# Planned attention and FP4 feed-forward block on one core: shifted due times, a split planned in four jobs, value eviction moved to ScalarE, paired mask matmuls

## The chip, the core and the metric

The kernel runs on one core of a Trainium2 chip. The metric is the device time of one execution in microseconds (us), as a median over runs. Engines: PE is TensorE's matmul, PEld its weight load, DVE is VectorE, ACT is ScalarE, POOL is GpSimd, SP is SyncE (here the only issuer of DMAs, each engine working through its own list in order).

## What is computed

One transformer block with adaptive layer norm, for x of 16 batches x 1024 tokens x 256 features in float32. Cut to what matters:

```
sa, ca, ga, sb, cb, gb = split(silu(c) @ wmod)          # per batch, |ga|,|gb| >= 0.25
h = layernorm(x) * (1 + ca) + sa
Q, K, V = h @ q_w.T + q_b, h @ k_w.T + k_b, h @ v_w.T + v_b   # 16 heads of 16
p = softmax(Q K / 4 + slope_h * (k - q), causal)
x = x + ga * ((p @ V) @ o_w.T + o_b)
h = layernorm(x) * (1 + cb) + sb
g = silu(fp4(h) @ fp4(w_gate).T) * (fp4(h) @ fp4(w_up).T)     # 704 wide
x = x + gb * (fp4(g) @ fp4(w_down).T)                         # fp4: blocks of 16, quantised and back
```

Since the rows of a softmax sum to 1, a constant added to V comes out of the attention unchanged.

## The kernel before

**One list per engine, written by a planner.** `plan()` names every job of all 16 batches: its engine, a cost, a due time, what it comes after, and a lag until others see it. `settle()` places them one by one: of all jobs that are ready it takes the one with the smallest pair (start, due), where the start is the later of the engine's free time and the job's own, but at least the free time plus 0.05, so that jobs that can start within 0.05 us are ranked by due time. The result, `PLAN.order`, is what each engine's `run()` walks through, in order, with semaphore waits. Nothing is decided on the chip. Batches overlap: in the stretch in which batch b is in attention, the projections of b+1 and the feed-forward of b-1 run as well. The length of a batch in due times is L = 240.

**Rings.** TensorE's results go through rings to the engine that evicts them: ring A to ACT (up to 4 jobs ahead), ring D to DVE (3 ahead), and Q passes quantised tiles from DVE to POOL (2 ahead). The evictor takes them in the order in which TensorE filled them. `RINGS`, `APART`, `BANKS` and `AHEAD` stand at the head of class Plan. `APART` names the DVE jobs that the planner does not start while a POOL job is under way, and the other way round (`memory` in `settle()`).

**The jobs of one batch.** TR and U (L730, L738) transpose the normed x and project it to q and k in four units u; ACT evicts a U into xa (L888). POOL splits each unit into three bf16 parts (`split`, L970 to L976: high part, rest, middle part, last part, four instructions of 128x1024 that wait for one another) as one job SPL of cost 6.5. SP moves the parts into the rows of qa and ka (MOVE, L561). V (L769) projects the values in two halves of 128x1024; **DVE** evicts each by four 128x256 additions of `bv_row` into `va` (L1161), and `va_ready` tells TensorE. S (L713) computes scores with queries on the partitions, 22 jobs for each of four groups g of four heads, and DVE takes the row maxima (L1101 for several heads at once, L1103 for one). SM, MT and TOP turn the maxima into three more rows of qa. T (L673) computes the scores again, transposed, ACT takes their exponential into one of three slots of `arena` (L874), and PV (L690) multiplies them with va. A T or S job whose block holds the diagonal adds the causal mask by a matmul of the identity with a mask of 128 columns: L676 behind each head of a T job, L718 behind each head of an S job. T jobs hold one, two or four heads (at 512 or 384, 256 and 128 columns); with four, one 512-column mask goes first (L669). S jobs of the second query tile (qt = 1) hold four heads of 256 columns, side by side, each with a mask of its own; those of qt = 2 and 3 two heads, in a bank each. CO (L853) evicts the sums; DEN, NUM, RDW and RBC are DMAs, RD (L1127) DVE's reciprocal of the sums, MUL (L1018) POOL's normalising. O (L781) is the output projection with weights scaled by ga (WG, L993); OB (L989) scales the bias `bo_row` by ga, and FOLD adds it to x. In the feed-forward, per pair of tiles r: LN, XR, XQ on DVE (L1186 to L1077), XQ on POOL (L1008, L1011), XT; per tile t: GA with silu on ACT (L800, L912), UP (L807, L1213), HR and HQ on DVE (L1066 to L1077), HQ on POOL, HT, DN (L823, L1219), RES. SP waits for MT before it issues TOP (L565).

Of the kernel before, what the change touches and what calls it, by code (L numbers as in the profile page):

```python
# [19 lines left out]
G = 4  # L20
# [60 lines left out]
class Plan:  # L81
# [6 lines left out]
    APART = ("LN", "XR", "XQ", "HR", "HQ", "N3", "SM", "WQ", "QROW")  # L88
# [6 lines left out]
    def add(self, engine, event, cost, due, *after, lag=0.06, ring=None, takes=None, lock=None, banks=0, holder=None):  # L95

        self.jobs[engine, event] = (cost, due, [a for a in after if a], lag, ring, takes, lock, banks)
        if banks:  # L100
            self.holder[event] = holder or (self.RINGS[ring][1], event)

    def settle(self):
# [30 lines left out]
        while ready:  # L134
            best = None
            places = {n: place(n) for n in (1, 2)}
            for key in ready:
# [22 lines left out]
                rank = (max(t, start + 0.05), due)  # L160
# [36 lines left out]
def plan():  # L197
# [9 lines left out]
    def projections(b, at):  # L207
# [13 lines left out]
        for u in range(4):  # L221
            for hf in range(2):
# [6 lines left out]
            p.add("POOL", ("SPL", b, u), 6.5, due, ("ACT", ("U", b, u, 0)), ("ACT", ("U", b, u, 1)),  # L229
                  ("POOL", ("SPL", b, u - 1)) if u else ("POOL", ("SPL", b - 1, 3)), *free)  # L230
        for u, g in ((0, 0), (1, 0), (0, 1), (1, 1), (2, 2), (3, 2), (2, 3), (3, 3)):
            p.add("SP", ("MOVE", b, u, g), 3.9, at + (g + 1) * L / NG, ("POOL", ("SPL", b, u)),
                  ("PE", ("T", b - 1, g, NS - 1, jobs_of(NS - 1) - 1)), ("SP", ("TOP", b - 1, g + 1)) if g + 1 < NG else None, lag=6.0)
        for v in range(2):
            pe(("V", b, v), 3.5, at + L, ("ACT", ("TR", b, 0, 1)), ("ACT", ("TR", b, 1, 1)),
               ("ACT", ("T", b - 1, NG - 1, NS - 1, jobs_of(NS - 1) - 1)), ("PE", ("V", b, 0)) if v else None, ring="D", on="DVE",
               takes_cost=1.75, banks=2, then=(("PE", ("PV", b - 1, NG - 1, NS - 1)),))

    def maxima(b, at):
        n, last = 0, ("PE", ("S", b - 1, NG - 1, NT - 1))  # L240
        for g in range(NG):
            for j, (qt, _, heads) in enumerate(TILES):
                w = (qt + 1) * P
                due = at + L * n / (NG * sum(h * (q + 1) * P for q, _, h in TILES)) - 30.0
                pe(("S", b, g, j), 0.65 if qt == 0 else heads * (cols(w) + 0.11) if w <= BANK else cols(BANK) + cols(w - BANK), due, last,
# [12 lines left out]
    def attention(b, at):  # L258
        n, last = 0, ("PE", ("T", b - 1, NG - 1, NS - 1, jobs_of(NS - 1) - 1))
        for g in range(NG):  # L260
            for s in range(NS):
                w = span(s)[1]
                heads = together(s)
                for i in range(jobs_of(s)):
                    due = at + L * n / (NG * NS * G)
                    old = b * NG * NS + n // G - P_SLOTS
                    pe(("T", b, g, s, i), 0.63 if heads == G else heads * (cols(w) + (0.1 if s in DIAGONAL else 0.0)) + 0.01, due, last,
# [7 lines left out]
                      ("PE", ("PV", b, g, s - 1)) if s else None, ("DVE", ("V", b, 1)) if (g, s) == (0, 0) else None, lag=0.22,  # L275
# [18 lines left out]
    def weights():  # L294
# [15 lines left out]
    def residual(b, at):  # L310

        p.add("SP", ("GROW", b), 0.7, at, ("POOL", ("WG", b - 1)), lag=3.0)
        p.add("POOL", ("OB", b), 0.75, at + 10.0, ("SP", ("GROW", b)), ("POOL", ("FOLD", b - 1, NPAIR - 1)))
# [63 lines left out]
def adaln_block(nc, x, wq, bq, wk, bk, wv, bv, wo, bo, w_gu, w_down, cond, w_mod, out):  # L377
# [5 lines left out]
    with ExitStack() as ctx:  # L383
# [40 lines left out]
        bv_row, bo_row = sb("bv_row", [P, D]), sb("bo_row", [P, D])  # L424
# [36 lines left out]
        va_ready = sem("va_ready")  # L461
# [3 lines left out]
        xn_ready = sem("xn_ready")  # L465
# [31 lines left out]
        def _(sp):  # L497
# [14 lines left out]
            for dst, src in ((bv_row, bv), (bo_row, bo)):  # L512
                sp.dma_start(dst[:, :], src.broadcast_to((P, D))).then_inc(w_in[4], 16)
# [98 lines left out]
        def _(pe):  # L612
# [44 lines left out]
            def run():  # L657
                for e in PLAN.order["PE"]:
                    kind, b = e[0], e[1]
                    if kind == "T":  # L660
# [10 lines left out]
                        for m in range(heads):  # L671
                            h = j * heads + m
                            mm = pe.matmul(ps[:, m * w:(m + 1) * w], ka[g][0:KT, h, kt * P:(kt + 1) * P], qa[g][0:KT, h, q0:q0 + w],  # L673
                                           start=heads < G, stop=heads == G or s not in DIAGONAL, skip_group_check=True)
                            if s in DIAGONAL and heads < G:
                                mm = pe.matmul(ps[:, m * w:m * w + P], identb[:, :], maskT[:, :], start=False, stop=True,  # L676
                                               skip_group_check=True)
                        mm.then_inc(a_full, 1)
                    elif kind == "PV":
# [6 lines left out]
                        if g == 0 and s == 0:  # L686
                            pe.wait_ge(va_ready, b + 1)
# [6 lines left out]
                    elif kind == "S":  # L694
# [11 lines left out]
                        if qt == 0:  # L706
                            pe.matmul(ps[:, :], identb[:, :], triangle.unsqueeze(1).broadcast_to((P, G, P)),
                                      start=True, stop=False, skip_group_check=True)
                        for m in range(heads):
                            for a in range(0, w, BANK):  # L710
# [3 lines left out]
                                               ka[g][0:KS, h0 + m, a:z], start=qt > 0, stop=qt == 0 or heads == 1,  # L714
# [47 lines left out]
                    elif kind == "V":  # L762
# [4 lines left out]
                        for t in range(4):  # L767
                            for c in range(C):
                                mm = pe.matmul(ps[:, t * D:(t + 1) * D], featT[:, c, (4 * half + t) * P:(4 * half + t + 1) * P],  # L769
                                               wvT[:, c, :], start=(c == 0), stop=(c == C - 1))  # L770
                        mm.then_inc(d_full, 1)
# [60 lines left out]
        def _(act):  # L832
# [10 lines left out]
            def run():  # L843
                for e in PLAN.order["ACT"]:
# [19 lines left out]
                    if kind == "T":  # L864
# [62 lines left out]
        def _(pool):  # L927
# [31 lines left out]
            def split(b, u):  # L959
                dst = parts[PART_SLOT[u]]  # L960
                if u == 3:
                    for g in (0, 1):
                        pool.wait_ge(part_in[0, g], b * 96 + 96)
                elif b:
                    old = (3, 1, 2)[u]
                    for g in (2 * (old // 2), 2 * (old // 2) + 1):
                        pool.wait_ge(part_in[old, g], b * 96)
                pool.wait_ge(a_free, max(in_a["U", b, u, hf] for hf in range(2)))
                done = b * 4 + u + 1
                nc.gpsimd.tensor_scalar(dst[:, 0, :], qk[u % 2], 1.0, 1.0, ALU.mult, ALU.mult).then_inc(high_done, 1)  # L970
                pool.wait_ge(high_done, done)
                nc.gpsimd.tensor_tensor(qk[u % 2], qk[u % 2], dst[:, 0, :], ALU.subtract).then_inc(rest_done, 1)
                pool.wait_ge(rest_done, done)
# [347 lines left out]
```

## Time and profile before

| | us |
|---|---|
| median of 3 runs (3885.79 to 3888.7) | 3885.8 |
| the profiled execution, its own time | 3883.8 |
| its span, first to last instruction | 3881.4 |
| PE busy | 3570.4 (92%) |
| DVE busy | 3109.8 (80%) |
| ACT busy | 1902.2 (49%) |
| POOL busy | 1285.0 (33%) |

A matmul's busy time runs to the modelled end of its result, and matmuls overlap, so start-to-start times say more of TensorE's pace than durations. "Idle before" is what ended an engine's idle time just before a group. The mean granted TensorE clock was 0.98 of full speed.

### The profile page before, as it was taken

Reading aid. Unit: us, or ns where it says so; the run is one execution under the profiler, and the core shown is the slowest. Engines: PE = TensorE matmul, PEld = TensorE weight load, DVE = VectorE, ACT = ScalarE, POOL = GpSimd, SP = SyncE. Lnnn points to the kernel's source line nnn. Section 1 sums busy time; section 2 is a strip of 40 time slices with the busy share of each in tenths; the row PEclk is TensorE's granted clock in tenths of the full one; section 3 lists DMA queues with packets and bytes.
Section 4 is the critical chain, followed back from the end, with each engine's and each line's share of the span. In section 5 each row is a group of like instructions: output and inputs, shape, how many; then the busy total and the mean of one; then the engine's idle time right before and its main releaser. Section 6 shows DMA issues by size and latency. Waiting matters only on the chain.

```text
span 3881.4 us, 57828 instructions
## 1 busy us (share of the span) xinstructions
PE 3570.4 (92%) x21300; PEld 1882.3 (48%) x21300; DVE 3109.8 (80%) x6061; ACT 1902.2 (49%) x3471; POOL 1285.0 (33%) x918
## 2 busy tenths in 40 slices
PE   5999999999999999999999999999999999999967
PEld 2334454544555554455544555455455545444435
DVE  9888779788887878879787887878878787877745
ACT  2455545455554545545445444554545454554521
POOL 5214234142332414324242332514334242332223
PEclk7899999999999999999999999999999999999988
DMA  7251323332342331333332242332333233232000
GB/s 125 35 95 34 67 48 53 61 48 49 55 66 49 59 57 35 65 55 52 57 55 48 49 70 48 56 60 38 60 56 58 49 61 52 39 61 39 20 25 11
DMA packets 158188, 205.51 MB, mean 53 GB/s; under 512 B 44036, under 2 KB 98004, under 8 KB 157908
## 3 DMA queue, kind: packets, MB, share of 16 engines
q1 hardware_dynamic: 157908, 201.82, 30.7%
q8 instruction: 170, 2.79, 0.3%
q14 instruction: 110, 0.90, 0.1%
HBM read 63.78 MB, written 17.89 MB: 21 GB/s over the span
## 4 chain that ended last, share of the span: by engine, by line
PE 68%; DVE 15%; ACT 9%; issue 3%; DMA 3%; SPq 3%; POOL 0%; POOLq 0%; ACTq 0%; DVEq 0%
PE banks L690 12%; PE banks L713 10%; PE banks L673 10%; PE banks L800 7%; PE banks L823 7%; PE banks L807 7%; ACT arena L874 6%; DVE banks L1103 3%; PE banks L738 3%; PE banks L781 3%; PE banks L769 3%; SPq L561 2%; DMA sums<-oT 2%; PE banks L816 2%; PE banks L676 2%
## 5 line engine op out<-in xcount | busy, mean ns | idle before, releaser
L874 ACT ACTIVATE arena<-banks 128x512 f32<-128x512 f32 (+1 forms) x2432 | 1274.4, 582 | 1008.1 <-PE banks L676 597.0
L1103 DVE CUSTOM_DVE_ANT_0 banks<-banks,mask 128x640 f32<-128x640 f32 (+3 forms) x1024 | 1033.3, 1043 | 123.7 <-PE banks L713 115.1
L673 PE MATMUL banks<-qa,ka 105*128 105x512 bf16 (+3 forms) x3072 | 817.0, 329 | 119.9 <-ACT arena L874 100.2
L713 PE MATMUL banks<-ka,qa 102*128 102x512 bf16 (+3 forms) x3072 | 753.0, 331 | 38.6 <-DVE top L1103 18.6
L690 PE MATMUL banks<-arena,va 128*17 128x512 f32 (+3 forms) x6144 | 643.7, 493 | 18.8 <-ACT arena L874 15.2
L673 PEld LDWEIGHTS banks<-qa,ka 105*128 105x128 bf16 x3072 | 279.7, 97 | 684.4 <-ACT arena L874 436.0
L1008 POOL TENSOR_TENSOR hid<-hid,tm 128x704 f32<-128x704 f32 x128 | 214.6, 1677 | 727.5 <-DVE hid L1077 727.5
L1101 DVE TENSOR_REDUCE top<-banks 128x2 f32<-128x768 f32 (+3 forms) x384 | 387.6, 1040 | 79.8 <-PE banks L718 75.8
L713 PEld LDWEIGHTS banks<-ka,qa 102*128 102x128 bf16 x3072 | 260.0, 99 | 379.0 <-DVE top L1103 106.6
L823 PE MATMUL banks<-wdT,hqT 128*128 128x256 f32 x1536 | 368.4, 391 | 2.8 <-ACT hqT L917 2.8
L1022 POOL TENSOR_TENSOR xr<-xr,delta 128x256 f32<-128x256 f32 x128 | 103.7, 810 | 675.7 <-DVE delta L1219 675.7
L800 PE MATMUL banks<-wguT,xqT 128*128 128x352 f32 x1024 | 326.7, 463 | 0.7 <-ACT xqT L908 0.7
L807 PE MATMUL banks<-wguT,xqT 128*128 128x352 f32 x1024 | 326.3, 464 | 0.0
L823 PEld LDWEIGHTS banks<-wdT,hqT 128*128 128x128 f32 x1536 | 292.5, 194 | 66.8 <-ACT hqT L917 9.7
L676 PE MATMUL banks<-maskT,identb 128*128 128x128 bf16 x1536 | 320.1, 220 | 0.0
L807 PEld LDWEIGHTS banks<-wguT,xqT 128*128 128x128 f32 x1024 | 191.4, 191 | 107.9 <-issue 5.4
L1213 DVE TENSOR_TENSOR hid<-hid,banks 128x704 f32<-128x704 f32 x128 | 112.8, 886 | 158.0 <-PE banks L807 157.3
L800 PEld LDWEIGHTS banks<-wguT,xqT 128*128 128x128 f32 x1024 | 189.7, 191 | 94.7 <-ACT arena L874 2.6
L912 ACT ACTIVATE hid<-banks 128x352 f32<-128x352 f32 x256 | 117.2, 463 | 237.6 <-PE banks L800 236.9
L690 PEld LDWEIGHTS banks<-arena,va 128*17 128x17 f32 x6144 | 104.2, 95 | 237.7 <-ACT arena L874 127.3
L1008 POOL TENSOR_TENSOR xb<-xb,tm 128x512 f32<-128x512 f32 x64 | 81.5, 1273 | 353.2 <-DVE xb L1077 353.2
L917 ACT COPY hqT<-banks 128x512 f32<-128x512 f32 (+1 forms) x256 | 110.9, 489 | 161.8 <-PE banks L816 161.8
(146 smaller groups left out, 4703.8 us busy)
## 6 DMA issues: line engine op xcount, KB each, us to landing
qa<-parts SPq DMA_DIRECT2D x384, 128.0 KB, 4.5
ka<-parts SPq DMA_DIRECT2D x384, 128.0 KB, 5.2
xa<-in_x SPq DMA_DIRECT2D x16, 1024.0 KB, 9.9
rsumT<-rsum_dram SPq DMA_DIRECT2D x64, 256.0 KB
onT<-oT SPq DMA_DIRECT2D x256, 64.0 KB, 4.3
xr<-in_x SPq DMA_DIRECT2D x64, 256.0 KB, 2.7
out_x<-xr SPq DMA_DIRECT2D x64, 256.0 KB, 2.2
ffn_rows<-rows_dram SPq DMA_DIRECT2D x16, 384.0 KB, 7.3
```

The source lines that it names most:

```text
L673: mm = pe.matmul(ps[:, m * w:(m + 1) * w], ka[g][0:KT, h, kt * P:(kt + 1) * P], qa[g][0:KT, h, q0:q0 + w], start=heads < G, stop=heads == ...
L676: mm = pe.matmul(ps[:, m * w:m * w + P], identb[:, :], maskT[:, :], start=False, stop=True, skip_group_check=True)
L690: mm = pe.matmul(out[32 * h:32 * h + VW, :], va[:, kt, g * G + h, :], probs[:, s % P_SLOTS, h, 0:w], start=s in FIRST, stop=s in LAST, ski ...
L713: mm = pe.matmul(ps[:, at:at + z - a], qa[g][0:KS, h0 + m, qt * P:(qt + 1) * P], ka[g][0:KS, h0 + m, a:z], start=qt > 0, stop=qt == 0 or h ...
L800: mm = pe.matmul(ps[:, 0:FH], src[:, c, :], wguT[:, c, e[3] * FH:(e[3] + 1) * FH], start=(c == 0), stop=(c == C - 1))
L807: mm = pe.matmul(ps[:, k * BANK:k * BANK + FH], src[:, c, :], wguT[:, c, FF + k * FH:FF + (k + 1) * FH], start=(c == 0), stop=(c == C - 1))
L823: mm = pe.matmul(ps[:, 0:D], hqT[t % 2][:, c, :], wdT[:, c, :], start=(c == 0), stop=(c == FC - 1))
L874: nc.scalar.activation(probs[:, s % P_SLOTS, j * heads:(j + 1) * heads, 0:w], ps[:, 0:heads * w].rearrange("p (h q) -> p h q", h=heads), A ...
L912: nc.scalar.activation(hid[t % 2][:, k * FH:(k + 1) * FH], ps[:, 0:FH], ACT.Silu).then_inc(a_free, 1)
L1008: nc.gpsimd.tensor_tensor(u, u, m, ALU.subtract).then_inc(gridded, 1)
L1101: nc.vector.tensor_reduce(tops, ps, AX.X, ALU.max).then_inc(d_free, 1)
L1103: nc.vector.tensor_tensor_reduce(out=ps, in0=ps, in1=mask[:, S - w:S], scale=1.0, scalar=MASKED, op0=ALU.add, op1=ALU.max, accum_out=tops) ...
```

## The change

It has five parts. (1) A table `SHIFT` adds a constant to the due time of each kind of job on each engine, and `PATIENCE` replaces the 0.05 in the rank: 0 on PE and DVE, 0.8 on ACT, 0.05 on POOL, 0.3 on SP. (2) N2 and LR (the two reciprocal-root chains) join `APART`. (3) POOL's split is planned as four jobs of one instruction each, so that others may stand between them. (4) V goes through ring A: ACT evicts each half by one 128x1024 copy, without the bias; the bias goes once, at the start, through the output projection (BB copies the bias column into `delta[0]`, BO multiplies it with o_w, DVE adds the result to `bo_row`), and OB of batch 0 waits for that. PV waits for ACT's copy itself; `va_ready` is gone. (5) The masks of two heads that lie side by side in a bank are one 256-column matmul: in T jobs of two heads, and for heads in pairs in S jobs of qt = 1. Only the first matmul of such a pair or job starts a new accumulation.

```
-    APART = ("LN", "XR", "XQ", "HR", "HQ", "N3", "SM", "WQ", "QROW")
+    APART = ("LN", "XR", "XQ", "HR", "HQ", "N2", "N3", "LR", "SM", "WQ", "QROW")
+    SHIFT = {"ACT CO": 12.0, "ACT GA": -20.0, "ACT HT": -16.0, "ACT T": -12.0, "ACT TR": 22.0, "ACT U": 11.0,
+             "ACT XT": 16.0, "DVE DN": 1.0, "DVE HQ": -14.0, "DVE LN": 12.0, "DVE LR": -24.0, "DVE N1": 1.0, "DVE N2": -1.0,
+             "DVE N3": 8.0, "DVE O": -3.0, "DVE RD": 17.0, "DVE S": -20.0, "DVE SM": -21.0, "DVE XQ": 11.0, "DVE XR": -22.0,
+             "PE DN": 10.0, "PE GA": 32.0, "PE HT": -7.0, "PE TR": 21.0, "PE U": 4.0, "PE UP": -7.0, "PE V": 1.0,
+             "PE XT": 9.0, "POOL FOLD": -2.0, "POOL HIGH": 13.0, "POOL HQ": 4.0, "POOL MID": -26.0, "POOL MUL": -6.0,
+             "POOL RES": 8.0, "POOL REST": -6.0, "POOL SPL": -2.0, "POOL WG": 8.0, "POOL XQ": 1.0, "SP MOVE": 10.0,
+             "SP NUM": -1.0, "SP OUT": -4.0, "SP RDW": 25.0, "SP XIN": 14.0}
+    PATIENCE = {"ACT": 0.8, "POOL": 0.05, "SP": 0.3}
...
+        due += self.SHIFT.get(engine + " " + event[0], 0.0)
...
-                rank = (max(t, start + 0.05), due)
+                rank = (max(t, start + self.PATIENCE.get(key[0], 0.0)), due)
...
-            p.add("POOL", ("SPL", b, u), 6.5, due, ("ACT", ("U", b, u, 0)), ("ACT", ("U", b, u, 1)),
+            p.add("POOL", ("HIGH", b, u), 1.1, due, ("ACT", ("U", b, u, 0)), ("ACT", ("U", b, u, 1)),
                   ("POOL", ("SPL", b, u - 1)) if u else ("POOL", ("SPL", b - 1, 3)), *free)
+            p.add("POOL", ("REST", b, u), 2.2, due, ("POOL", ("HIGH", b, u)))
+            p.add("POOL", ("MID", b, u), 1.1, due, ("POOL", ("REST", b, u)))
+            p.add("POOL", ("SPL", b, u), 2.2, due, ("POOL", ("MID", b, u)))
...
-               ("ACT", ("T", b - 1, NG - 1, NS - 1, jobs_of(NS - 1) - 1)), ("PE", ("V", b, 0)) if v else None, ring="D", on="DVE",
-               takes_cost=1.75, banks=2, then=(("PE", ("PV", b - 1, NG - 1, NS - 1)),))
+               ("ACT", ("T", b - 1, NG - 1, NS - 1, jobs_of(NS - 1) - 1)), ("PE", ("V", b, 0)) if v else None, ring="A", on="ACT",
+               takes_cost=1.15, banks=2, then=(("PE", ("PV", b - 1, NG - 1, NS - 1)),))
...
+        p.add("DVE", ("BB", 0), 0.4, 30.0)
+        pe(("BO", 0), 0.95, 40.0, ("DVE", ("BB", 0)), ring="D", on="DVE", takes_cost=0.45)
...
# TensorE, a T job
-                                           start=heads < G, stop=heads == G or s not in DIAGONAL, skip_group_check=True)
-                            if s in DIAGONAL and heads < G:
-                                mm = pe.matmul(ps[:, m * w:m * w + P], identb[:, :], maskT[:, :], start=False, stop=True,
-                                               skip_group_check=True)
+                                           start=heads < G and m == 0, stop=heads == G or s not in DIAGONAL, skip_group_check=True)
+                        if s in DIAGONAL and heads < G:
+                            mm = pe.matmul(ps[:, 0:heads * w].rearrange("p (h q) -> p h q", h=heads)[:, :, 0:P], identb[:, :],
+                                           maskT[:, :].unsqueeze(1).broadcast_to((P, heads, P)), start=False, stop=True,
+                                           skip_group_check=True)
...
# TensorE, an S job
+                        paired = 2 if qt == 1 else 1
...
+                            if heads > 1 and qt > 0 and m % paired == paired - 1:
+                                at = (m + 1 - paired) * tile_pitch(heads, w)
+                                mm = pe.matmul(ps[:, at:at + paired * w].rearrange("p (h k) -> p h k", h=paired)[:, :, w - P:w], identb[:, :],
+                                               triangle.unsqueeze(1).broadcast_to((P, paired, P)), start=False, stop=True,
                                                skip_group_check=True)
-                            if heads > 1 and qt > 0:
-                                at = m * tile_pitch(heads, w) + w - P
-                                mm = pe.matmul(ps[:, at:at + P], identb[:, :], triangle, start=False, stop=True, skip_group_check=True)
...
# ScalarE
+                    if kind == "V":
+                        t = 4 * e[2]
+                        if b:
+                            act.wait_ge(pv_done, b * NG * NS)
+                        act.wait_ge(a_full, full)
+                        nc.scalar.copy(va[:, t:t + 4, :, 0:HD], ps.rearrange("p (t h w) -> p t h w", t=4, h=H)).then_inc(a_free, 1)
...
# VectorE
-                        for j in range(4):
-                            ins = nc.vector.tensor_tensor(va[:, t + j, :, 0:HD], ps[:, j, :, :],
-                                                          bv_row[:, :].rearrange("p (h w) -> p h w", h=H), ALU.add)
...
+                        nc.vector.tensor_tensor(bo_row[:, :], bo_row[:, :], bank(e)[:, 0:D], ALU.add).then_inc(d_free, 1)
```

## Rows read from the trace of the kernel before

**Rows 1.** The page: busy time, share of the span and instructions of each engine

```profile
PE 3570.4 (92%) x21300; PEld 1882.3 (48%) x21300; DVE 3109.8 (80%) x6061; ACT 1902.2 (49%) x3471; POOL 1285.0 (33%) x918
```

**Rows 2.** Windows; columns: stretch, length, busy of PE, PEld, DVE, ACT, POOL, PEclk, DMA share, GB/s

```profile
0.00:484.00 484.00, 410.14 (x2360) 188.93 (x2360) 404.31 (x879) 228.17 (x398) 154.13 (x110) 0.92 0.40 71
484.00:3388.00 2904.00, 2749.50 (x16665) 1457.85 (x16666) 2381.33 (x4585) 1478.96 (x2708) 992.58 (x703) 1.00 0.32 54
3388.00:3881.40 493.40, 410.72 (x2277) 235.53 (x2276) 324.18 (x599) 195.11 (x367) 138.30 (x105) 0.93 0.16 31
```

**Rows 3.** Windows of 50 us, the two of the first 1000 us that are compared

```profile
250.00:300.00 50.00, 49.52 (x364) 23.95 (x361) 38.48 (x76) 30.66 (x61) 5.73 (x5) 1.00 0.60 99
...
950.00:1000.00 50.00, 49.16 (x330) 29.40 (x329) 36.23 (x71) 23.65 (x44) 9.43 (x8) 1.00 0.38 63
```

**Rows 4.** The chain that ended last, shares of the span by engine

```profile
PE 68%; DVE 15%; ACT 9%; issue 3%; DMA 3%; SPq 3%; POOL 0%; POOLq 0%; ACTq 0%; DVEq 0%
```

**Rows 5.** Waits: engine, line, waited for: us in total, times, longest us

```profile
PEld banks L673 <- ACT arena L874: 436.0, 684, 2.1
...
PEld banks L690 <- ACT arena L874: 127.3, 342, 1.1
...
PEld banks L713 <- DVE top L1103: 106.6, 147, 3.1
...
DVE rsums L1127 <- DMA sums<-oT: 66.5, 38, 3.7
...
DVE va L1161 <- PE banks L769: 57.0, 30, 3.3
```

**Rows 6.** Groups of PE matmuls by form (busy, mean ns | idle before)

```profile
L823 PE MATMUL banks<-wdT,hqT 128*128 128x256 f32 x1536 | 368.4, 391 | 2.8 <-ACT hqT L917 2.8
...
L676 PE MATMUL banks<-maskT,identb 128*128 128x128 bf16 x1536 | 320.1, 220 | 0.0
L718 PE MATMUL banks<-mask,identb 128*128 128x128 bf16 x768 | 161.6, 222 | 0.0
```

**Rows 7.** Timeline of PE: start us, us, what, count

```profile
1116.14 2.75 PE L823 MATMUL banks<-wdT,hqT 128*128 128x256 f32 x12
1118.73 2.53 PE L800 MATMUL banks<-wguT,xqT 128*128 128x352 f32 x8
...
1128.04 0.27 PE L713 MATMUL banks<-ka,qa 102*128 102x256 bf16 x1
1128.15 0.22 PE L718 MATMUL banks<-mask,identb 128*128 128x128 bf16 x1
1128.21 0.27 PE L713 MATMUL banks<-ka,qa 102*128 102x256 bf16 x1
```

**Rows 8.** Groups: DVE's value eviction, and ACT's copies in two sizes

```profile
L1161 DVE TENSOR_TENSOR va<-banks,bv_row 128x256 f32<-128x256 f32 x128 | 45.3, 417 | 57.0 <-PE banks L769 57.0
...
L917 ACT COPY hqT<-banks 128x512 f32<-128x512 f32 x128 | 75.7, 591 | 161.8 <-PE banks L816 161.8
...
L917 ACT COPY hqT<-banks 128x256 f32<-128x256 f32 x128 | 49.6, 388 | 0.1
```

**Rows 9.** Two DVE lines: group (mean ns), then duration ns min/median/max of the same

```profile
L1073 DVE SCALAR_TENSOR_TENSOR hid<-hid,invH 128x704 f32<-128x704 f32 x128 | 143.6, 1122 | 1.9
...
L1108 DVE SCALAR_TENSOR_TENSOR top_rest<-top,top_parts 128x32 f32<-128x32 f32 x64 | 38.5, 602 | 2.2
...
L1073 DVE SCALAR_TENSOR_TENSOR hid<-hid,invH x128: 883/891/2737, 344.0 to 3864.3; 128x704 f32<-128x704 f32 x128
...
L1108 DVE SCALAR_TENSOR_TENSOR top_rest<-top,top_parts x64: 191/193/2304, 104.3 to 3670.0; 128x32 f32<-128x32 f32 x64
```

**Rows 10.** Timeline of POOL and of DVE at one place

```profile
1098.07 2.27 POOL L972 TENSOR_TENSOR xa<-xa,parts 128x1024 f32<-128x1024 f32 x1
1098.40 2.69 DVE L1077 TENSOR_TENSOR hid<-hid,tm 128x704 f32<-128x704 f32 x1
```

**Rows 11.** Waits of SP's queue: waited for, us in total, times, longest us

```profile
SPq L565 <- DVE topT L1120: 957.5, 64, 39.0
```

More of the change, by code:

```diff
@@ L266, in attention @@
                     old = b * NG * NS + n // G - P_SLOTS
-                    pe(("T", b, g, s, i), 0.63 if heads == G else heads * (cols(w) + (0.1 if s in DIAGONAL else 0.0)) + 0.01, due, last,
+                    pe(("T", b, g, s, i), 0.63 if heads == G else heads * cols(w) + (0.11 if s in DIAGONAL else 0.01), due, last,
                        ("SP", ("TOP", b, g)) if (s, i) == (0, 0) else None, ring="A", on="ACT",
@@ L770, in run @@
                                                wvT[:, c, :], start=(c == 0), stop=(c == C - 1))
+                        mm.then_inc(a_full, 1)
+                    elif kind == "BO":
+                        ps = open_banks(e)
+                        pe.wait_ge(bv_ready, 1)
+                        for c in range(C):
+                            mm = pe.matmul(ps[:, 0:D], delta[0][:, c * P:(c + 1) * P], woT[:, c, :], start=(c == 0), stop=(c == C - 1))
                         mm.then_inc(d_full, 1)
@@ L957, in _ @@
             nc.gpsimd.memset(wdT[:, FC - 1, :], 0.0).then_inc(pad_clear, 1)
[L959 to L973, printed above, removed]
-                nc.gpsimd.tensor_scalar(dst[:, 1, :], qk[u % 2], 1.0, 1.0, ALU.mult, ALU.mult).then_inc(mid_done, 1)
-                pool.wait_ge(mid_done, done)
-                nc.gpsimd.tensor_tensor(dst[:, 2, :], qk[u % 2], dst[:, 1, :], ALU.subtract).then_inc(split_done, 1)
             def run():
@@ L980, in run @@
                     kind, b = e[0], e[1]
-                    if kind == "SPL":
-                        split(b, e[2])
+                    if kind in ("HIGH", "REST", "MID", "SPL"):
+                        u = e[2]
+                        dst, src, done = parts[PART_SLOT[u]], qk[u % 2], b * 4 + u + 1
+                        if kind == "HIGH":
+                            if u == 3:
+                                for g in (0, 1):
+                                    pool.wait_ge(part_in[0, g], b * 96 + 96)
+                            elif b:
+                                old = (3, 1, 2)[u]
+                                for g in (2 * (old // 2), 2 * (old // 2) + 1):
+                                    pool.wait_ge(part_in[old, g], b * 96)
+                            pool.wait_ge(a_free, max(in_a["U", b, u, hf] for hf in range(2)))
+                            nc.gpsimd.tensor_scalar(dst[:, 0, :], src, 1.0, 1.0, ALU.mult, ALU.mult).then_inc(high_done, 1)
+                        elif kind == "REST":
+                            pool.wait_ge(high_done, done)
+                            nc.gpsimd.tensor_tensor(src, src, dst[:, 0, :], ALU.subtract).then_inc(rest_done, 1)
+                        elif kind == "MID":
+                            pool.wait_ge(rest_done, done)
+                            nc.gpsimd.tensor_scalar(dst[:, 1, :], src, 1.0, 1.0, ALU.mult, ALU.mult).then_inc(mid_done, 1)
+                        else:
+                            pool.wait_ge(mid_done, done)
+                            nc.gpsimd.tensor_tensor(dst[:, 2, :], src, dst[:, 1, :], ALU.subtract).then_inc(split_done, 1)
                     elif kind == "OB":
```

42 lines of the change are left out of this document (18 added, 24 removed).

## The prediction

> **What bounds the kernel now.** I read the busy shares first [rows 1]: PE 92%, DVE 80%, ACT 49%, POOL 33%. Nothing but TensorE is near its limit, yet DVE is close enough that delays on it can show. Then the windows by stage [rows 2]: in the 2904 us of the steady middle PE is busy 2749.5 us, 94.7%, at the full 2.4 GHz clock (granted 1.00); the first 484 us and the last 493.4 us hold 410 us of PE work each, so the two ends lose about 157 us (484.0 - 410.1 + 493.4 - 410.7) and the middle 154.5 us. The clock falls at the ends alone (0.92, 0.93), where TensorE waits most. The chain that ended last [rows 4] says the same: PE 68%, DVE 15%, ACT 9%, and no POOL. So TensorE's stream sets the time, with gaps where its next job in the fixed order has to wait.
>
> What are those gaps? In the waits [rows 5] the weight loads of the T jobs wait for ACT's exponential 684 times (436.0 us), those of PV 342 times, those of S for DVE's maxima 147 times. ACT is only half busy, so these waits come from the order: exponentials come in bursts, and a TensorE job that could run stands behind one that can't. There is a second kind of loss, on DVE. The same instruction on the same shape takes 891 ns at the median and up to 2737 (L1073); one of 32 elements takes 193 at the median and up to 2304 (L1108) [rows 9]. At one place the timeline shows such a one, 2.69 us of L1077, beside a GpSimd instruction of the split of 2.27 us [rows 10]: DVE ended 0.72 us after GpSimd. For two groups alone the excess over the median is 128 x (1.122 - 0.891) = 29.6 us and 64 x (0.602 - 0.193) = 26.2 us [rows 9]. DVE also waits 66.5 us in 38 waits for the DMA of the sums, with maxima queued behind the reciprocal [rows 5].
>
> The Trainium skill (SBUF — State Buffer, Who interferes with whom) states that GpSimd and a DVE instruction with two SBUF inputs or in a 2-port mode hold one shared port pair exclusively, so that the later one fully blocks. Here the trace agrees, with 2304 ns where 193 is usual.
>
> **The change part by part.** The sum is made against the profiled execution, 3883.8 us (span 3881.4 and 2.4 around it), 2.0 us under the median of 3885.8.
>
> *Paired masks.* A T job of two heads exists for 2 steps x 2 jobs x 4 groups x 16 batches = 256, and loses one mask matmul each; an S job of qt = 1 exists 64 times and loses two. So 384 of the 2304 mask matmuls [rows 6] go, but their columns stay: two of 128 become one of 256. Their 220 ns are mostly overlap; the cost is start to start. A mask takes 0.06 us (1128.15 to 1128.21), a 256-column bf16 matmul 0.11 (1128.04 to 1128.15) [rows 7]. Each pairing saves 0.12 - 0.11 = 0.01 us: -4 us. Bounds: 0, and one whole mask, 384 x 0.06 = -23 us. I take the value between matmuls of the very width.
>
> *Values on ACT.* 128 DVE additions of 417 ns go, 45.3 us, and with them the 57.0 us that DVE stood waiting for the projection [rows 8, 5]. ACT gets 32 copies of 128x1024. No row has this size; from the copies of 256 and 512 columns, 388 and 591 ns, each 256 more cost 203 ns, so one takes 591 + 2 x 203 = 997 ns: 31.9 us (bounds 20, if it ran at two thirds of that, and 38, at two copies of 591 ns). TensorE's work is the same. On the path I count by the chain's shares [rows 4]: -45.3 x 0.15 = -6.8, +31.9 x 0.09 = +2.9, together -4 us. Bounds: all of the 45.3 us gained, or the copy and its wait all exposed on ACT, +89 us (the rival below).
>
> *Bias through the projection.* One copy, two matmuls and one addition, once, in a stretch where DVE is busy for 404 of 484 us [rows 2]; a broadcast load of 128 rows becomes a load of one column. OB of batch 0 comes 40 us and more after it. 0 us; without that cover at most the length of the four, about 2 us.
>
> *The split in four jobs.* The same four GpSimd instructions with the same waits. Others may now stand between them, so the moves of the parts can be later by one GpSimd job for each unit; at 2.27 us [rows 10] and 64 units that is 145 us if all of it were exposed, nothing at the other end. I take 0: POOL is a third busy, and in the long waits of TensorE [rows 5] neither the split nor a DMA is the releaser. Behind a late move on SP's queue stand TOP, sums and output stores; SP itself stands 957.5 us in 64 waits for the copy of the maxima before TOP [rows 11], so it has time, but no liberty of order.
>
> *Due times, patience, two more kinds apart.* No instruction is added. What moves is the order on all five lists. Three things are visible in the table. S on DVE and PE: DVE's S is due 20 earlier, RD 17 later, so the reciprocal no longer stands ahead of maxima the moment its DMA is thought landed; that addresses the 66.5 us. LR and N2 are kept from GpSimd, and the planner now knows where each of the split's instructions ends and DVE may begin; that addresses the blocked DVE time. GA on PE is 32 later, so that feed-forward matmuls, which ACT need not answer at once, are left for places where the attention waits. For RDW (+25) and MOVE (+10) the later place is paid by slack on SP. ACT's patience of 0.8 us touches only CO and KROW, since the rest of its list is fixed by the ring: 128 x 0.8 = 102 us at most, 0 taken at 49% busy.
>
> How much is it worth? The trace has no row of another order. Bounds: below, nothing; above, every stretch as dense as the two best, 49.52 and 49.16 us of 50 [rows 3], 98.7%: 2904 - 2749.5 / 0.987 = 118 us. These stretches do the same work with the same engines, so the level is reachable, but not with any mix of jobs. I take the middle of the two occupancies, 96.7%: 2904 - 2749.5 / 0.967 = 61 us. A choice, not a measurement; it is also half of the DVE losses named above (66.5 + 29.6 + 26.2 = 122 us). At the ends I take nothing: at the start weights are quantised, and at the end the last feed-forward runs alone, a chain that no order shortens much.
>
> Sum: 3883.8 - 4 - 4 - 61 = 3814.8, and 2.0 for the median: **3817 us**. The case's own range holds all times at which the order finds 16 to 108 of the 118 us: 3862 down to 3770 (from 3886 - 8 = 3878).
>
> **The rivals.**
>
> *Denser than the busy share allows for.* Twelve matmuls of L823 take 1118.73 - 1116.14 = 2.59 us, 216 ns each [rows 7], while their mean duration is 391 [rows 6]. So behind each wait some 175 ns are counted busy in which nothing streams. For the 1173 waits of the three rows named above that is 205 us more of true idle time. If the new order ends a quarter of them (51 us) and reaches the dense level (118), the time is 3886 - 8 - 118 - 51 = 3709; with the level alone 3760. Around 3735. For it: DVE has 122 us of named losses to give as well; against it: it asks for the best level on every stretch, and some of the waits are a matmul's own result coming back. The Trainium skill (Perfetto Trace Analysis, Identifying the Most-Contended Engine) says that matmul busy time is no measure of the distance to the roofline, since matmuls are pipelined; by that rule the room is the larger one, and the 216 against 391 ns agree.
>
> *The order buys nothing on the chip.* Waits only change places: a blocked DVE instruction depends on where both engines really are, and the plan's times drift against the chip's. Then 3886 - 8 = 3878, between 3862 and 3893.
>
> *Slower, by ACT's queue.* In the old kernel the wait for the value projection stood on DVE, 30 waits of 1.9 us [rows 5]; it now stands on ACT, and the exponentials of the new batch's first group are queued behind it, for which TensorE's T and PV jobs wait already 1026 times. Price: 57.0 + 31.9 = 89 us on ACT. With an order that gives nothing, half of it exposed gives 3886 - 4 + 45 = 3927. It decides as soon as more than about 12 us of the 89 (0.4 us a copy) reach TensorE and the order gives nothing, or more than 73 if the order gives its 61. For it: ring A is in order and TensorE's longest waits are on it. Against: ACT idles half of the time, and O, TR and feed-forward matmuls stand near.
>
> **How the numbers follow.** A measurement of this kernel can tell about 0.2%, 7.8 us, from no change. Chances: forecast 0.52, denser 0.18, order buys nothing 0.15 (its centre lies on the 0.2% bound, so half of it is faster and half the same), slower 0.15. Faster: 0.52 + 0.18 + 0.07 = 0.77. Same: 0.08. Slower: 0.15. The range goes from 3730, which takes in the level alone and the forecast's own span and leaves out the lower half of the denser case, to 3895, which takes in the case of no gain and leaves out most of the slower one.
>
> **What would show it.** In the changed profile: 384 fewer mask matmuls (1920 left), with PE busy lower by more than 4 us only if gaps went; DVE busy lower by 45 us for the values and more if blocked instructions went (maxima of L1073's and L1108's kind near their medians less often); DVE's wait for the sums below 20 us; V's copy on ACT near 1.0 us, and its wait for L769 under 2 us each; PE busy in the steady middle between 96 and 98%. Wrong: a steady occupancy under 95%, T's waits on ACT over 436 us, or new waits of TensorE on DMAs of the parts, which would say that the split is late. If the gain lies in the first and last 490 us, the step that gave the ends nothing is wrong.

## The result: 3706.5 us, 4.7% faster, outside the predicted range

The changed kernel takes 3706.53 us (median of 4 runs, 3703.08 to 3707.59) against 3885.8: a ratio of 0.9534, 95% interval 0.9522 to 0.9546, so 179 us. Forecast were 3817, with 3730 to 3895 as the range. The direction was right, the forecast gain of 69 us less than half of what came, and the time lies 23 us below the range.

The page of the changed kernel, busy time and the chain that ended last (they answer to [rows 1] and [rows 4]):

```profile
PE 3520.1 (95%) x20920; PEld 1879.2 (51%) x20920; DVE 3027.4 (82%) x5935; ACT 1912.3 (52%) x3503; POOL 1286.7 (35%) x918
...
PE 84%; DVE 10%; ACT 3%; issue 2%; POOL 1%; DMA 0%; SPq 0%; ACTq 0%; POOLq 0%; DVEq 0%
```

The chain is TensorE's now, 84% instead of 68%. PE's busy time fell by 50 us, though 384 pairings can't take more than a few. The rest must be the modelled ends of matmuls behind which waits went: the kernel at the end of the experiments, with the same 21300 matmuls as before and only another order, has 3514.3 us, 56 less. The windows of the changed kernel, columns as in [rows 2]:

```profile
0.00:484.00 484.00, 414.58 (x2397) 196.70 (x2398) 418.61 (x884) 236.92 (x415) 155.47 (x110) 0.92 0.42 71
484.00:3200.00 2716.00, 2654.91 (x16036) 1425.49 (x16034) 2253.71 (x4399) 1456.49 (x2674) 969.20 (x687) 0.99 0.33 57
3200.00:3700.90 500.90, 450.60 (x2490) 257.01 (x2489) 355.12 (x655) 218.94 (x414) 161.99 (x122) 0.94 0.18 35
```

PE is busy 97.8% of the middle (2654.91 of 2716), 94.7% before. For the share of each stage, the output projection O is a mark in every batch. TensorE's timeline of the kernel before, at the first O, at the 5th and 14th, and at the last two:

```profile
308.63 7.17 PE L781 MATMUL banks<-wog,onT 128*128 128x256 f32 x32
...
1228.56 7.17 PE L781 MATMUL banks<-wog,onT 128*128 128x256 f32 x32
...
3313.89 7.17 PE L781 MATMUL banks<-wog,onT 128*128 128x256 f32 x32
...
3545.19 7.17 PE L781 MATMUL banks<-wog,onT 128*128 128x256 f32 x32
...
3744.17 8.53 PE L781 MATMUL banks<-wog,onT 128*128 128x256 f32 x32 [19.23 <-issue]
```

and of the changed kernel, the same five:

```profile
304.89 7.12 PE L806 MATMUL banks<-wog,onT 128*128 128x256 f32 x32
...
1179.45 7.07 PE L806 MATMUL banks<-wog,onT 128*128 128x256 f32 x32
...
3173.73 7.07 PE L806 MATMUL banks<-wog,onT 128*128 128x256 f32 x32
...
3392.47 7.07 PE L806 MATMUL banks<-wog,onT 128*128 128x256 f32 x32
...
3573.97 10.06 PE L806 MATMUL banks<-wog,onT 128*128 128x256 f32 x32 [3.73 <-issue]
```

A batch took (3313.89 - 1228.56) / 9 = 231.7 us and takes (3173.73 - 1179.45) / 9 = 221.6. Of the 180.5 us between the spans, 3.7 lie before the first O, 149.0 in the 14 batches to the 15th O, 17.5 in the interval to the last O (TensorE's idle time before it is 3.73 us instead of 19.23), and 10.3 behind it. With the shares of the middle, a batch's 10.1 us are 7.3 of idle time (12.3 to 5.0) and 2.8 of busy time. The waits, as [rows 5], with the new one of ACT for the values:

```profile
PEld banks L688 <- ACT arena L905: 194.2, 299, 1.6
...
PEld banks L706 <- ACT arena L905: 111.0, 315, 1.1
...
ACT va L894 <- PE banks L788: 99.9, 31, 15.5
...
PEld banks L730 <- DVE top L1135: 92.9, 114, 2.0
...
DVE rsums L1159 <- DMA sums<-oT: 32.4, 16, 4.2
```

T waited for ACT 684 times and waits 299 times; the waits of PV for ACT and of S for the maxima changed little (111.0 us from 127.3, 92.9 from 106.6). S waits for ACT more often than before, 146 times instead of 78:

```profile
PEld banks L713 <- ACT arena L874: 32.9, 78, 0.9
...
PEld banks L730 <- ACT arena L905: 90.6, 146, 0.9
```

(L713 in the kernel before is L730 in the changed one.) The profile says what ended, not which part of the change ended it.

### The profile page after: what moved, and what is told of

The parts are those of the page before. It is cut to its first block, busy times and chain, and to the rows that moved or that the text cites. A ratio compares the mean times of both kernels' runs of the same rounds, so it can differ in the third digit from the quotient of the medians.

```text
span 3700.9 us, 56917 instructions
## 1 busy us (share of the span) xinstructions
PE 3520.1 (95%) x20920; PEld 1879.2 (51%) x20920; DVE 3027.4 (82%) x5935; ACT 1912.3 (52%) x3503; POOL 1286.7 (35%) x918
## 4 chain that ended last, share of the span: by engine, by line
PE 84%; DVE 10%; ACT 3%; issue 2%; POOL 1%; DMA 0%; SPq 0%; ACTq 0%; POOLq 0%; DVEq 0%
PE banks L706 14%; PE banks L688 13%; PE banks L730 13%; PE banks L825 8%; PE banks L832 8%; PE banks L848 7%; PE banks L757 5%; PE banks L806 3%; PE banks L788 3%; DVE banks L1135 2%; PE banks L841 2%; PE banks L691 2%; ACT arena L905 2%; DVE tm L1108 1%; PE banks L735 1%
## 5 line engine op out<-in xcount | busy, mean ns | idle before, releaser
L730 PE MATMUL banks<-ka,qa 102*128 102x512 bf16 (+3 forms) x3072 | 761.0, 332 | 55.0 <-DVE top L1135 40.2
L688 PE MATMUL banks<-qa,ka 105*128 105x512 bf16 (+3 forms) x3072 | 791.1, 330 | 17.5 <-ACT arena L905 7.0
L688 PEld LDWEIGHTS banks<-qa,ka 105*128 105x128 bf16 x3072 | 270.4, 98 | 480.8 <-ACT arena L905 194.2
L730 PEld LDWEIGHTS banks<-ka,qa 102*128 102x128 bf16 x3072 | 258.7, 99 | 430.9 <-DVE top L1135 92.9
L691 PE MATMUL banks<-maskT,identb 128*128 128x128 bf16 (+1 forms) x1280 | 298.2, 233 | 0.0
L706 PEld LDWEIGHTS banks<-arena,va 128*17 128x17 f32 x6144 | 102.6, 95 | 232.0 <-ACT arena L905 111.0
L1005 POOL TENSOR_SCALAR parts<-xa 128x1024 bf16<-128x1024 f32 x64 | 79.2, 1237 | 395.3 <-ACT xa L919 301.6
L1043 POOL TENSOR_TENSOR hid<-hid,scaleH 128x704 f32<-128x704 f32 x128 | 177.5, 1387 | 10.0
```

Of the source, the lines that this page charges most:

```text
L691: mm = pe.matmul(ps[:, 0:heads * w].rearrange("p (h q) -> p h q", h=heads)[:, :, 0:P], identb[:, :], maskT[:, :].unsqueeze(1).broadcast_to ...
L706: mm = pe.matmul(out[32 * h:32 * h + VW, :], va[:, kt, g * G + h, :], probs[:, s % P_SLOTS, h, 0:w], start=s in FIRST, stop=s in LAST, ski ...
L730: mm = pe.matmul(ps[:, at:at + z - a], qa[g][0:KS, h0 + m, qt * P:(qt + 1) * P], ka[g][0:KS, h0 + m, a:z], start=qt > 0 and m % paired == ...
```

## The experiments

Theory A: the due times carry the gain. Theory B: work taken off DVE and TensorE does. Within A: is it one entry, and by what path? Ratios are to runs of the kernel before on the same chip, with the 95% interval in brackets.

**The four other parts without the table.** Edit to the changed kernel:

```
-    SHIFT = {"ACT CO": 12.0, ...}
+    SHIFT = {}
-    PATIENCE = {"ACT": 0.8, "POOL": 0.05, "SP": 0.3}
+    PATIENCE = {"PE": 0.05, "DVE": 0.05, "ACT": 0.05, "POOL": 0.05, "SP": 0.05}
```

> The changed kernel with SHIFT empty and the old rank (0.05 on every engine): values on ACT, split in four jobs, paired masks and two more kinds apart stay. Theory A (the due times carry the gain): a few us to 30 us under the kernel before, 3850 to 3880, with TensorE's waits of T for ACT above 600. Theory B (work taken off DVE and off TensorE carries it): 3700 to 3760.

Measured: 3888.8 us, ratio 0.9995 [0.9986, 1.0004]. Values on ACT, the finer split, paired masks and the two more kinds apart together are worth nothing with the old rank, less than either theory gave them. T waits for ACT 593 times.

**The table on the old work.** The kernel before, with the change's `SHIFT`, its `PATIENCE` and the two lines that use them:

> The kernel before with only the table SHIFT and PATIENCE added; values on DVE, split as one job, single masks. Theory A, if the table works on any set of jobs: 3700 to 3780. Theory A', if it fits only the set it was made for: 3800 to 3870. Theory B: 3850 or more.

Measured: 3858.9 us, ratio 0.9919 [0.9906, 0.9933]. So neither half does it: 0 and 31 us, but 179 together. Either the two need each other, or the table fits the set it stands with.

**The masks.** The changed kernel's lists, with the mask matmuls one by one:

```
-                        paired = 2 if qt == 1 else 1
+                        paired = 1
...
-                            mm = pe.matmul(ps[:, 0:heads * w].rearrange("p (h q) -> p h q", h=heads)[:, :, 0:P], identb[:, :],
-                                           maskT[:, :].unsqueeze(1).broadcast_to((P, heads, P)), start=False, stop=True,
+                                mm = pe.matmul(ps[:, m * w:m * w + P], identb[:, :], maskT[:, :], start=False, stop=True,
```

> The changed kernel's lists unchanged, with the instructions of the masks as before (384 matmuls of 128 columns more). The prediction's step: +4 us (3710). The upper bound of that step, a whole mask each: +23 us.

Measured: 3709.4 us, ratio 0.9537 [0.9524, 0.9550], 2.8 us above the change; the intervals overlap, so the size can be told neither from 4 us nor from nothing.

**Values back on DVE; the split as one job again.** The first puts V on ring D with four copies on DVE, the second makes one job of 6.5 of HIGH, REST, MID and SPL. The table stays in both.

```
-               ... ring="A", on="ACT",
-               takes_cost=1.15, banks=2, then=(("PE", ("PV", b - 1, NG - 1, NS - 1)),))
+               ... ring="D", on="DVE",
+               takes_cost=1.75, banks=2, then=(("PE", ("PV", b - 1, NG - 1, NS - 1)),))
...
+                        for j in range(4):
+                            ins = nc.vector.tensor_copy(va[:, t + j, :, 0:HD], ps[:, j, :, :])
```

> The changed kernel with the values evicted by DVE again (four copies of 128x256 for each half, ring D; the bias still goes through the projection), with the same table. Theory V (moving 45 us of DVE work is what makes room for the order): 3790 or more, most of the gain gone. The prediction's step (values worth about 4 us): 3705 to 3720. Theory I (parts and table are worth something only together, since the table was made for this set): 3740 to 3800.

> The changed kernel with the split planned as one job of 6.5 us again, same instructions. The prediction's step (0): 3700 to 3712. Theory P (jobs between the split's instructions let GpSimd's quantising follow DVE sooner): 3725 to 3760.

Measured: 3709.9 us, ratio 0.9542 [0.9527, 0.9556], and 3704.0 us, 0.9528 [0.9514, 0.9542]. Each is the time of the change within the intervals. Of the parts undone one at a time, none matters. The two more kinds in `APART` and the path of the bias were not undone alone.

**One entry out: the gate.** `SHIFT` without `"PE GA": 32.0`.

> The changed kernel without the one entry 'PE GA': 32. Theory G (the later gate matmuls, kept for places where attention waits, are most of the due-time gain): more than half of the 180 us is lost, 3800 to 3860, and TensorE's waits of T for ACT rise from 299 towards 684. Theory M (the gain is spread over many entries): 3720 to 3760.

Measured: 3879.6 us, ratio 0.9974 [0.9965, 0.9983]: one of 43 constants, and 173 us of the 179 are gone, more than either theory allowed (where the expectations count the other entries, they count two too few). But T's waits for ACT rise only to 450 (273.9 us). The rest shows in another place. Windows of 5 us of this kernel:

```profile
2275.00:2280.00 5.00, 5.00 (x34) 1.43 (x32) 4.97 (x9) 4.61 (x10) 1.13 (x1) 1.00 0.80 147
2280.00:2285.00 5.00, 0.91 (x9) 0.57 (x6) 3.89 (x5) 0.34 (x1) 4.23 (x4) 1.00 0.17 58
2285.00:2290.00 5.00, 5.00 (x17) 3.31 (x16) 3.65 (x5) 2.93 (x4) 1.26 (x1) 0.66 0.23 56
```

Columns are as in [rows 2]. TensorE is idle for 4 us, and in the next 5 us its granted clock is 0.66, a mean of its two levels, so a good part of that stretch runs at 1.2 GHz. The timeline at that place says what it waited for:

```profile
2278.87 2.36 POOL L1044 TENSOR_TENSOR onT<-onT,rsumT 128x1024 f32<-128x1024 f32 x1 [8.30 <-DMA rsumT<-rsum_dram]
...
2281.19 0.72 POOL L1048 TENSOR_TENSOR xr<-xr,delta 128x256 f32<-128x256 f32 x1
2281.87 1.26 POOL L1034 TENSOR_TENSOR xb<-xb,tm 128x512 f32<-128x512 f32 x1
...
2283.21 1.10 POOL L1037 TENSOR_TENSOR xb<-xb,scaleX 128x512 f32<-128x512 f32 x1
...
2284.45 0.63 PE L810 MATMUL banks<-ident,xb 128*128 128x128 f32 x4 [4.09 <-POOL xb L1037]
```

GpSimd stood 8.30 us for the DMA of the reciprocals with MUL at the head of its list. RES and the quantising XQ stood behind it, and TensorE's XT, next in its own list, stood behind XQ.

**That one place alone.** The kernel without the gate's entry, and in 12 of the batches GpSimd's MUL moved behind RES and XQ. TensorE's, DVE's, ACT's and SP's lists are the same:

```
 PLAN = plan()
+for b in range(1, B):
+    late, quick = ("MUL", b, 0), ("XQ", b - 1, 2)
+    pool = PLAN.order["POOL"]
+    if 0 < pool.index(quick) - pool.index(late) <= 3:
+        pool.remove(late)
+        pool.insert(pool.index(quick) + 1, late)
```

> The kernel without the gate's entry (3880) with one job moved: in 12 batches GpSimd's MUL stands behind RES and XQ instead of ahead of them; every other list is the same. Theory Q (MUL stands waiting for the DMA of the reciprocals and holds GpSimd's quantising, on which TensorE's transposes XT and the gate matmuls wait; the clock falls with it): the waits of XT for GpSimd (41.5 us in 11) vanish, the granted clock of the middle rises from 0.98, and the time falls by 5 to 8 us a batch, to 3780 to 3820. Theory T (the gate entry works through TensorE's own order of T and gate jobs alone): 3870 to 3885.

Measured: 3807.2 us, ratio 0.9795 [0.9780, 0.9809]. 72 us for one job moved by two places (70 by the two ratios), 6.0 us a batch. XT's waits for GpSimd fell from 13 (55.5 us in all) to 1 (12.7 us), so the waits themselves are 42.8 us of it. The mean granted clock of the whole run rose from 0.966 to 0.974 (medians of the runs), which over 3880 us is some 31 us more, an estimate; together 74. The windows of the middle, first without the entry,

```profile
484.00:3300.00 2816.00, 2667.35 (x15706) 1419.09 (x15704) 2302.23 (x4307) 1432.32 (x2624) 931.70 (x672) 0.98 0.32 53
```

then with MUL moved:

```profile
484.00:3300.00 2816.00, 2705.60 (x16142) 1437.32 (x16140) 2351.38 (x4423) 1471.04 (x2691) 958.04 (x691) 0.99 0.33 55
```

In the same time 436 matmuls more, and in this stretch XT no longer waits for GpSimd. So 72 of the 173 us are lost by GpSimd's list and a DMA, without a change in TensorE's order. The other 101 are the order of the five lists at large; which places they are in was not taken apart.

The bad place isn't one that the gate's entry had to cure in the kernel before. In the lists that `plan()` writes for the kernel before and for the changed one, the XQ in question (the third pair of the batch in feed-forward) stands ahead of the first MUL, by 6 and by 9 places in nearly every batch; only with the other 42 entries and without the gate's does it stand 2 behind in 12 batches.

**The gate's entry alone.** `SHIFT = {"PE GA": 32.0}`, the rest of the changed kernel as it is.

> The changed kernel with 'PE GA': 32 as the only entry. With the gate entry worth 174 us on top of the 40 others and the 40 others worth 9 us without it, it alone gives anything from 3720 (the entry is the cause) to 3850 (only together). Since XQ and MUL then lie otherwise on GpSimd, a wait of XT for GpSimd in the trace would put it at the upper end.

Measured: 3787.3 us, ratio 0.9742 [0.9723, 0.9761]. With the four other parts and the change's `PATIENCE`, the entry gives 101 us over the kernel with no table; the 42 others give 9 without it and 81 on top of it. The 9 hide the collision: with MUL moved, the 42 without the gate give 79 us (3807.2 against 3886.3 for the kernel before). 101 and 79 are 180, the whole gain, so apart from that one place the gate's entry and the others hardly need each other. What `PATIENCE` gives alone was not measured.

**TensorE's entries alone.** The eight entries of PE, without the 35 others:

> The changed kernel with the entries of PE alone kept in the table (DN 10, GA 32, HT -7, TR 21, U 4, UP -7, V 1, XT 9); the 33 others are gone. If TensorE's own order carries the gain: 3720 to 3760. If the DVE entries (S -20, RD 17, LR -24) are needed as the prediction named them: 3800 or more.

Measured: 3786.1 us, ratio 0.9737 [0.9723, 0.9752], between the two theories. The same as the gate's alone: TR, UP, DN and the others of PE add nothing to it. 80 us come with the entries of the other four engines.

**One entry out: the reciprocal.** `SHIFT` without `"DVE RD": 17.0`.

> The changed kernel without the entry 'DVE RD': 17. The prediction's step on the reciprocal: DVE's wait for the sums rises from 32 us towards the 66 us of before, and the time by about half of that, 3715 to 3730. If one entry can upset the whole order, as the gate's did: 3780 or more.

Measured: 3769.0 us, ratio 0.9687 [0.9668, 0.9707], 62 us lost, again between the two theories. The path that I had named isn't it: DVE's wait for the sums is 21.9 us here, less than with the entry. The timeline of this kernel shows what came instead, once in every batch of the middle, some 21 us behind the start of O:

```profile
1666.30 3.14 DVE L1204 SCALAR_TENSOR_TENSOR xb<-xr,mv,ffn_rows 128x256 f32<-128x256 f32 x2
...
1666.98 2.18 POOL L1002 TENSOR_TENSOR xa<-xa,parts 128x1024 f32<-128x1024 f32 x1
...
1669.48 3.40 DVE L1209 SCALAR_TENSOR_TENSOR xb<-xb,rs,ffn_rows 128x256 f32<-128x256 f32 x2
...
1670.43 2.17 POOL L1008 TENSOR_TENSOR parts<-xa,parts 128x1024 bf16<-128x1024 f32 x1
...
1673.93 0.45 PE L724 MATMUL banks<-ka,qa 102*128 102x512 bf16 x2 [2.93 <-DVE top L1127]
```

LN's four instructions, 0.48 us each at the median, take 6.5 us together since they lie beside the split, and TensorE stands 2.93 us behind the maxima that DVE couldn't take. From 484 to 3200 us this wait stands in the trace 12 times, 35.2 us in all; in the changed kernel it is missing there. It is the prediction's second loss, a DVE instruction held up beside one of GpSimd, and what stands behind it makes it cost. That it is the cause of the 62 us is argued and not shown: no run moved LN alone, and in its place the changed kernel has more waits of S for the other maxima (22, 35.3 us, against 13, 7.8 us here).

**Another table for the change, and one for the old work.** Both tables were found by trying changes of entries and keeping those that shorten the planner's own sum of costs, first for the changed kernel (52 entries and other patiences, nothing else), then for the kernel before with all its work as it was. The second differs from the kernel before in nothing but:

```
+    SHIFT = {"ACT CO": 206.0, ..., "PE DN": -4.0, "PE GA": 33.0, "PE HT": -8.0, ..., "PE TR": 21.0, "PE U": 4.0, "PE UP": -85.0, ...}
+    PATIENCE = {"ACT": 0.4, "DVE": 0, "PE": 0, "POOL": 0.3, "SP": 0}
...
+        due += self.SHIFT.get(engine + " " + event[0], 0.0)
...
-                rank = (max(t, start + 0.05), due)
+                rank = (max(t, start + self.PATIENCE.get(key[0], 0.0)), due)
```

> The changed kernel with another table of due times, found by trying changes of entries against the planner's own sum of costs. If TensorE's stream is the floor now (221 us a batch, of which some 5 idle): 3680 to 3706, a gain at the ends and of a us or two a batch at most. If drift between plan and chip decides: anything up to 3740.

> The kernel before, all its work as it was (values and their bias on DVE, one mask per head, the split as one job, N2 and LR not apart), with a table of due times found for this work in the way of the last one. Theory O (the order is all; the other four parts are worth their few us and the table of the change only fits the lists it was made for): 3700 to 3740. Theory W (values off DVE and the finer split are what a dense order needs): 3780 to 3850.

Measured: 3685.2 us for the change with another table (ratio 0.9480 [0.9464, 0.9496]), faster than both kernels, and 3687.7 us for the old work with its own (0.9499 [0.9477, 0.9521]), below both theories. This settles the question between A and B. With the values and their bias on DVE, single masks, the split as one job and the old `APART`, the order alone gives 198 us, more than the change. The two searched kernels lie 2.5 us apart, within the intervals, so the four other parts show no worth here either, as far as two searches can be compared. The middle of the old work with its own table, columns as in [rows 2]:

```profile
484.00:3200.00 2716.00, 2664.12 (x16439) 1453.75 (x16438) 2287.02 (x4535) 1441.12 (x2666) 975.61 (x692) 1.00 0.33 57
```

PE is busy 98.1% of it. The 31 us of the change's table on the old work were what a table gives that was made for another set of jobs.

## Why the prediction was wrong

**Right in kind.** TensorE's stream set the time and the gaps came from the order; the due times were the one term of weight. The masks (4 us forecast, 2.8 us with them undone), the values (4 forecast, 3.4 undone) and the split (0, and 2.6 us less with it undone) agree with the runs, but none of the three is clear of the noise. V's copy on ACT takes

```profile
L894 ACT COPY va<-banks 128x1024 f32<-128x1024 f32 x32 | 32.4, 1013 | 99.9 <-PE banks L788 99.9
```

1013 ns, where 997 were worked out from the two smaller copies. Its waits on ACT are 99.9 us, more than the 57.0 on DVE, and ACT carries them: the slower rival's place exists, with no price that a run shows. ACT is busy 52% of the span.

**Wrong in size: "I take the middle of the two occupancies, 96.7%: 2904 - 2749.5 / 0.967 = 61 us."** The order gave 149 us in the batches, with the few us of the other parts in it. Two things failed in the term. It and the bound above it, 118 us, took TensorE's busy time as fixed; that fell by 2.8 us a batch, and the kernel with the old work and only another order shows that it falls with the waits. The prediction had this (216 against 391 ns) in a rival and left it out of its sum. And the middle between two occupancies was taken for want of a reason. The measured 97.8% lies inside the 96 to 98% that the prediction gave as a sign of being right, and three quarters of the way from 94.7 to 98.7; the old work with its own table has 98.1%. The two dense windows were the better guide, though no table brought the whole middle to their level.

**A better number stood in the kernels.** `plan()` ends with the time at which its last engine is free (`PLAN.length`). It is 3945.8 us for the kernel before and 3745.8 for the changed one, 200 less, where 179 were measured; a part of this is that the changed planner takes paired masks to be cheaper. With the same work and costs, before and the last kernel of the experiments, it is 3945.8 and 3743.8, 202 less, where 198 were measured. For a single part it is no measure: with the values back on DVE it is 45.7 us longer and the chip 3.4.

**Wrong at the ends: "At the ends I take nothing."** They gave 31.5 us (3.7, 17.5 and 10.3). The 19.23 us of TensorE before the last O stood in the trace of before and were no part of what I gave as the reason, the quantising at the start and the last feed-forward.

**Wrong in the path of RD.** The entry is worth 62 us, and not through the 66.5 us of waits for the sums; without it LN meets the split and a new wait of 2.93 us comes in every batch of the middle, but how much of the 62 us that makes is open. And T's waits for ACT, the first loss that I named, don't follow the time: the kernel with the gate's entry alone has more of them (552, 330.6 us) than the one without the gate's entry (450, 273.9 us) and is 92 us faster. The blocked time on DVE changed its places more than it went. The two groups of [rows 9] in the changed kernel:

```profile
L1105 DVE SCALAR_TENSOR_TENSOR hid<-hid,invH 128x704 f32<-128x704 f32 x128 | 117.0, 914 | 3.5
...
L1140 DVE SCALAR_TENSOR_TENSOR top_rest<-top,top_parts 128x32 f32<-128x32 f32 x64 | 16.9, 264 | 2.2
```

Their excess fell from 55.8 to 7.5 us (128 x 0.023 + 64 x 0.071), yet DVE's busy time fell by 82.4 us in all, less than these 48.3 and the values' 45.3 together, so other instructions take longer than before. That 61 us is also half of the named DVE losses says nothing for the term.

The rival "denser than the busy share allows for", 3709 to 3760 with a chance of 0.18, is the nearest to what came, 2.5 us past its lower end. Its mechanism, idle and modelled busy time falling together, is in the trace; its number was in part luck. It gave the middle 118 + 51 = 169 us and the ends nothing, where the batches gave 149 and the ends 31.5. The Trainium skill's rule beside it (Perfetto Trace Analysis, Identifying the Most-Contended Engine), that matmul busy time is no measure of the distance to the roofline, agrees with the traces: the same 21300 matmuls are busy 3570.4 us in one order and 3514.3 in another.

Of the other signs, V's copy near 1.0 us and the 1920 mask matmuls came. Missed were the wait for the sums (32.4 us, forecast below 20) and the wait of V's copy (without the longest of 15.5 us it is 2.8 us each, forecast under 2). Two readings are slightly off, with no effect on the sum: in [rows 10] DVE ends 0.75 us after GpSimd and not 0.72, and two thirds of 31.9 us are 21 and not 20.

## What to carry to other kernels

In a kernel whose engines follow fixed lists, price an order by the engine that sets the time: take its stream start to start, not its busy share. Here two tables brought it to 97.8 and 98.1% busy in the middle, near the 98.7% of the densest stretches in the trace of before. If a planner wrote the lists, look at its own length for both orders. Undo each part with the order held, and search the order again for the old work, before crediting a part: here the plausible savings on DVE, GpSimd and TensorE were worth some 3 us each or nothing. One entry taken out of a fitted table can open a collision of its own, so its loss is no measure of its worth. And look in each in-order list for a job that is fed by a DMA and stands ahead of a short one on which others wait: in the kernel without the gate's entry, moving it by two places gave 2%.

## What the runs showed of the hardware

Twelve waits of TensorE, one in each of 12 batches and 42.8 us in all, cost 72 us (3879.6 against 3807.2 us). In the 5 us behind the one that is shown above, of 4.09 us, the granted clock was 0.66, between its two levels; over the middle it was 0.98 instead of 0.99.

The length of a wait alone doesn't say whether the clock falls. From 484 to 3200 us the kernel before has 149 matmul waits of T for ACT up to 1.2 us and 15 of S for the maxima up to 2.1 us, and ran at 1.00. The kernel with the gate's entry alone ran the middle at 1.00 too, with 12 waits of TensorE of 3.0 us on average and 3.7 at most. The changed kernel has no wait of a matmul above 1.7 us in its middle and ran it at 0.99; behind one of 1.66 us, at 1228.51, its windows show

```profile
1225.00:1230.00 5.00, 3.51 (x22) 1.84 (x20) 4.93 (x6) 1.02 (x3) 3.36 (x2) 1.00 0.01 2
1230.00:1235.00 5.00, 4.55 (x22) 1.52 (x23) 3.67 (x9) 1.69 (x3) 3.47 (x3) 0.66 0.02 3
```

What else decides it was not tested.

DVE instructions of 0.48 us at the median, LN's with two inputs, took up to 2.35 us; in the case shown, beside GpSimd instructions of 2.2 us, four of them took 4.6 us more than four medians.
